# Recurrent cell: the part copies of the key halves issued from GpSimd's queue, those of the query halves from SyncE's

## The reference, cut to what matters

```
log_f = jax.nn.log_sigmoid(fg)
cs = jnp.cumsum(log_f, axis=1)
log_D = where(mask, cs[:, :, None] - cs[:, None, :], -inf) + ig[:, None, :]
max_log_D = jnp.max(log_D, axis=-1, keepdims=True)
D_mat = jnp.exp(log_D - max_log_D)
qk = jnp.einsum('hsd,htd->hst', qh, kh) / np.sqrt(DH)
C = qk * D_mat
normalizer = jnp.maximum(jnp.abs(C.sum(axis=-1, keepdims=True)), jnp.exp(-max_log_D))
h = jnp.einsum('hst,htd->hsd', C / (normalizer + EPS), vh)
return (h - mu) / jnp.sqrt(var + LN_EPS) * ln_scale
```

## Time and profile before

| what | us |
|---|---|
| median of 3 runs | 6493.87 |
| lowest and highest of them | 6456.07 and 6500.29 |
| the profiled execution | 6481.38 |
| its span | 6479.7 |
| the cell stage in it, from GpSimd's first instruction to VectorE's last | 3149.1 to 3470.5 |

### The profile page before, as it was taken

The page is one execution under the profiler, slowest core; times in us unless marked ns, Lnnn a source line. Parts: engine busy times, 40 slices in busy tenths (PEclk is TensorE's granted clock), DMA queues, the critical chain, the costliest instruction groups (busy, mean ns, idle before and its releaser), DMA issues. The chain is left out here.

```text
span 6479.7 us, 102180 instructions
## 1 busy us (share of the span) xinstructions
PE 4692.1 (72%) x24710; PEld 2851.4 (44%) x24710; DVE 3959.5 (61%) x8261; ACT 2814.7 (43%) x5978; POOL 2018.5 (31%) x3020
## 2 busy tenths in 40 slices
PE   7446666391787973797675767697677687995897
PEld 4113333240353322687233645486555574333533
DVE  6335555637546876444387966557866455886565
ACT  2235555114314762322453556434556332772353
POOL 0114443000006641222343554124553113552342
PEclk9557889695897987898777989898889898997897
DMA  4999996100034330210452232002321006332543
GB/s 157 301 323 194 184 185 149 50 0 0 0 115 133 90 75 20 70 43 23 128 157 59 109 113 74 29 7 78 133 74 46 26 16 200 91 86 60 181 124 97
DMA packets 372621, 648.43 MB, mean 100 GB/s; under 512 B 78834, under 2 KB 182931, under 8 KB 372200
## 3 DMA queue, kind: packets, MB, share of 16 engines
q1 hardware_dynamic: 300728, 450.70, 22.9%
q0 software_dynamic: 71488, 193.32, 12.4%
HBM read 373.99 MB, written 238.70 MB: 95 GB/s over the span
## 5 line engine op out<-in xcount | busy, mean ns | idle before, releaser
L1115 DVE TENSOR_REDUCE t_nmax<-t_aps 128x2 f32<-128x1024 f32 x700 | 837.6, 1222 | 281.9 <-PE t_aps L1037 276.4
L1222 ACT ACTIVATE t_expT<-t_bps 128x512 f32<-128x512 f32 x1290 | 701.7, 599 | 288.2 <-PE t_bps L1056 237.8
L1056 PE MATMUL t_bps<-t_Q,t_K 51*128 51x512 f32 (+2 forms) x1290 | 528.9, 472 | 59.4 <-ACT t_expT L1222 43.3
L1037 PE MATMUL t_aps<-t_K,t_Q 49*128 49x512 f32 (+2 forms) x1400 | 467.7, 462 | 64.7 <-DMA t_K<-k_halves 29.4
L1056 PEld LDWEIGHTS t_bps<-t_Q,t_K 51*128 51x128 f32 (+2 forms) x1290 | 230.2, 190 | 528.6 <-ACT t_expT L1222 374.2
L2474 DVE TENSOR_TENSOR f_hl<-f_h,f_hh 128x512 fp32r<-128x512 f32 x192 | 203.9, 1062 | 412.4 <-ACT f_hh L2399 412.4
L3882 ACT ACTIVATE t_relsb<-t_relsb,t_nmax 128x128 f32<-128x128 f32 (+3 forms) x515 | 280.3, 561 | 317.4 <-DVE t_nmax L3855 314.1
L1083 PE MATMUL t_ops<-t_expT,t_V 128*17 128x512 f32 (+1 forms) x2560 | 416.6, 618 | 0.4 <-ACT t_expT L1222 0.4
L3816 PE MATMUL t_tps<-ident,t_relsb 128*128 128x128 f32 x1280 | 266.8, 317 | 173.5 <-ACT t_expT L3701 165.2
L2762 POOL TENSOR_TENSOR a_crossed<-a_qsb,a_tab 128x256 f32<-128x256 f32 x272 | 268.0, 1007 | 299.7 <-ACT a_qsb L2709 272.1
L3855 DVE CUSTOM_DVE_ANT_0 t_relsb<-t_sps,t_relsb 128x128 f32<-128x128 f32 (+3 forms) x515 | 235.5, 485 | 138.2 <-POOL t_relsb L3781 86.5
(11 more groups left out here) (431 smaller groups left out, 12493.6 us busy)
## 6 DMA issues: line engine op xcount, KB each, us to landing
rel<-r_out SPq DMA_DIRECT2D x128, 640.0 KB, 5.4
t_relsb<-rel SPq DMA_DIRECT2D x128, 256.0 KB, 4.6
t_Q<-q_halves POOLq DMA_DIRECT2D x420, 64.0 KB, 2.5
t_K<-k_halves POOLq DMA_DIRECT2D x420, 64.0 KB, 2.6
t_relsb<-rel SPq DMA_DIRECT2D x128, 192.0 KB, 3.6
k_halves<-a_parts SPq DMA_DIRECT2D x48, 512.0 KB
q_halves<-a_parts SPq DMA_DIRECT2D x48, 512.0 KB, 5.5
t_relsb<-rel SPq DMA_DIRECT2D x128, 128.0 KB, 3.5
```

The source lines that it names most:

```text
L1037: last = nc.tensor.matmul(aps[:, (t * PPG + i) % 2, x, :], operand(Qr, KA, p, h, slice(t * P, (t + 1) * P)), operand(Kr, KA, p, h, slice(0 ...
L1056: nc.tensor.matmul(bps[:, slot_of(kb, j), :], operand(Kr, KB, p, h, slice(kb * P, (kb + 1) * P)), operand(Qr, KB, p, h, slice(0, S)), star ...
L1115: nc.vector.tensor_reduce(nmax[:, g, t, i * HPT:(i + 1) * HPT], aps[:, (t * PPG + i) % 2], AX.X, ALU.max, negate=True).then_inc(s["maxed"], 1)
L1222: nc.scalar.activation(expT[:, kb % RING, j, :], bps[:, slot_of(kb, j), :], ACT.Exp).then_inc(s["expo"], 1 + (PAD if end else 0))
```

## The change

The twelve copies of a set that write `K` (8 of `Kh`, 4 of `Kl`) leave SyncE's queue for GpSimd's; the twelve that write `Q` stay. Each kind gets semaphores of its own (`parts0/1`, `kparts0/1`), and TensorE waits for both. GpSimd issues the copies of parts(b, 0) after `keys(b)` and ahead of the diagonal of pair 3, and those of parts(b, 1) after the diagonal and maxima of pair 0 and ahead of the diagonal of pair 1. ScalarE's `Qh` waits for the copies of Q alone, `Kh` and GpSimd's `Kl` for those of K alone.

```diff
-    PARTS = 6 * HH * 16
+    PARTS = 3 * HH * 16
...
-                    for made, dst, src, terms in (("qh", Q, Qh, (0, 1)), ("kh", K, Kh, (0, 2)), ("ql", Q, Ql, (2,)), ("kl", K, Kl, (1,))):
+                    for made, dst, src, terms in (("qh", Q, Qh, (0, 1)), ("ql", Q, Ql, (2,))):
...
                 def keys(b):
                     pool.wait_ge(s["kh"], b + 1)
-                    wait(pool, "parts1", b * PARTS)
+                    wait(pool, "kparts1", b * PARTS)
...
+                def parts(b, half):
+
+                    if b or half:
+                        wait(pool, "score", ((b - 1) * HP + 2 + 2 * half) * NT)
+                    for made, dst, src, terms in (("kh", K, Kh, (0, 2)), ("kl", K, Kl, (1,))):
+                        pool.wait_ge(s[made], b + 1)
+                        for j in range(HH):
+                            for r in terms:
+                                pool.dma_start(dst[r * DH:(r + 1) * DH, half, j, :], src[j * DH:(j + 1) * DH, half, :]).then_inc(s[f"kparts{half}"], 16)
...
                 keys(0)
+                parts(0, 0)
                 pool.wait_ge(s["tri"], 1)
                 for g in range(NP):
                     b, i = pair(g)
                     diagonal(g)
                     maxima(g + 2)
+                    if i == 0:
+                        parts(b, 1)
                     if i == 2 and b + 1 < NB:
                         queries(b + 1)
                         keys(b + 1)
+                        parts(b + 1, 0)
                     if i == 3 and b:
                         spread(b - 1)
...
                         pe.wait_ge(s[f"parts{i // 2}"], (b + 1) * PARTS)
+                        pe.wait_ge(s[f"kparts{i // 2}"], (b + 1) * PARTS)
...
-                    wait(act, "parts1", b * PARTS)
+                    wait(act, "kparts1", b * PARTS)
```

More of the change, by code:

```diff
@@ L2994, in cell @@
     RING = 3
-    PARTS = 6 * HH * 16
-    with phase(nc, name, "w c0 c1 qh kh ql kl parts0 parts1 vt vcp vones m0 m1 m2 diag d score ct zero pv kept turned lg den0 den1 den2 normed bn stats held rstd centred out tri tri0") as (s, sb, ps):
+    PARTS = 3 * HH * 16
+    with phase(nc, name, "w c0 c1 qh kh ql kl parts0 parts1 kparts0 kparts1 vt vcp vones m0 m1 m2 diag d score ct zero pv kept turned lg den0 den1 den2 normed bn stats held rstd centred out tri tri0") as (s, sb, ps):
         cT = sb("cT", [P, 2, KT, S])
```

## The result

| | kernel before | changed kernel |
|---|---|---|
| median, lowest and highest of 20 runs each | 6484.93 (6456.07 to 6514.83) | 6510.35 (6485.54 to 6544.65) |
| profiled execution, its span | 6481.38, 6479.7 | 6505.1, 6503.4 |
| cell stage in it | 321.4 | 337.0 |
| VectorE's wait between the stage and the next one | 1.83 | 8.33 |

The changed kernel takes 1.0041 times as long, 95% interval 1.0028 to 1.0054: some 27 us more, 18 to 35 by the interval. That is slower, but inside the 1% at which this text draws its line. 6510 was measured and 6512 predicted, but the agreement is largely luck. The forecast stood on a median of 3 runs of the kernel before, 6494, and 20 runs give 6485; so the baseline was 9 us too high and the step, +18 forecast and +25 measured by the medians, 7 us too small. And part of that step went where the prediction did not look.

The account below looks back on a forecast made before the run. The cell stage was taken as a ring of waits through SyncE's issues and GpSimd's queue. Turns +19.1, start +1.0 and end -2.2 made +18 us on a median of 6494: 6512 us, range 6467 to 6550.

Parts of the forecast that it names:

- What bounds the kernel: Cell stage: a chain of waits, with SyncE's issues (15.2 of 38.3 us a turn) and GpSimd's queue on the ring.
- The price of an issue: GpSimd's queue: 0.52 us for each copy issued, 6.2 us for a set of twelve.
- Rival B: GpSimd issues cost twice as much beside VectorE: +96 us on top of the +18, 6608 us; chance 0.08.
- The set for pairs 2 and 3: GpSimd, ahead of pair 1's diagonal: diagonal ready at T0+8.8, `Qh` at T0+15.4 instead of T0+16.6, 1.2 us left.
- T0: Moment when the last scores of a batch are done, which releases the next part copies; a turn runs between two.
- The set for pairs 0 and 1: GpSimd, ahead of the spread: it ends 16.8 us after `Qh`, VectorE idles 6.3, 25.2 us to next T0.
- rival C: The turn stays the same, VectorE or TensorE absorbing half the delay: 0 to +8 us, 6494 to 6502; chance 0.17.
- Sum of a turn: Batch cycle: 15.4 + 25.2 = 40.6 us against 38.3; six turns 243.6 us against 224.5, +19.1.
- The start: Before the first turn: last scores come at 3202.2, where SyncE began at 3201.2 before; +1.0 us.
- The end: Last batch, only its first half counting: pair 2 begins 2.2 us earlier, -2.2 us.
- Rival A: GpSimd's issues cost the ring nothing: 34.4 us a turn, -27 us, 6467 as a median; chance 0.15 (or between it and nothing).
- Beside the next diagonal, as before: VectorE's add behind the spread: taken as 3.6 us, unchanged, in the 25.2 us from `Qh` to the next T0.

Follow-up runs that it names:

- set0_behind_spread: Changed kernel with the K copies for pairs 0 and 1 issued after the spread instead of ahead of the diagonal of pair 3: 6470.0 us, ratio 0.9970.
- both_behind: Changed kernel with K copies for pairs 0 and 1 after the spread, those for pairs 2 and 3 after the diagonal of pair 1: 6452.26 us, ratio 0.9942.
- after_drain_earlier: Changed kernel with one more DRAIN on GpSimd, in idle time ahead of the last batch's spread: 6506.05 us, ratio 1.0021.
- set1_behind_diagonal: Changed kernel with the K copies for pairs 2 and 3 issued after the diagonal of pair 1 and ahead of the maxima: 6511.28 us, ratio 1.0025.
- both_behind_drain_earlier: both_behind with one more DRAIN on GpSimd ahead of the last batch's spread: 6451.91 us, ratio 0.9933 against the kernel before.
- set1_alone_behind_drain_earlier: Changed kernel, only K copies for pairs 2 and 3 on GpSimd, behind pair 1's diagonal; the others on SyncE; early DRAIN: 6466.77 us, ratio 0.9954.
- k_copies_left_out: Changed kernel with the copies of `Kh` and `Kl` made for batch 0 only: 6452.71 us in one run.

## Why the prediction was right, and where it was not

*What bounds the kernel*: right. The stage is a ring of waits, GpSimd's queue lies on it with almost no slack, and what stands ahead of the diagonal and of the spread is paid for. set0_behind_spread and both_behind show it by moving nothing but the order.

*The price of an issue*: 0.496 us (median) against 0.52, a set 5.9 us against 6.2. Rival B is out: the longest took 0.535, beside VectorE's work. The note of the Trainium skill that the prediction named there (SBUF — State Buffer, the note on DVE blocking DMAs under SBUF: two separate sides) did not bear on these issues by its own condition, and none of the 192 shows such a wait.

*The set for pairs 2 and 3*: diagonal ready and pair 1 begun at T0+8.7 (8.8 predicted), `Qh` at T0+15.1 (15.4). "The old wait is gone" and "what is late next is ScalarE" both hold.

*The set for pairs 0 and 1*: the spread ends 16.1 us after `Qh` (16.8), the tiny operation of the divide is at 0.17 us as said, T0 follows 24.5 us after `Qh` (25.2). The idle time of the add is 8.39 us, not 6.3: the centre ran beside issues and took 1.66 us instead of 3.43, so VectorE was early by that much and waited it out. This was in rival C as a gain. It is none, because the add waits for `rstd` anyway.

*Sum of a turn*: 39.6 us, 40.6 predicted. The six turns took 3440.14 - 3199.73 = 240.4 us, +15.9 instead of +19.1. Five are of 39.6 and one of 42.3: the gap before GpSimd's 129th DMA lies in it. So the turns were 1.0 us shorter than forecast each, and a stop that I did not foresee gave 2.7 us of that back: luck once more.

*The start*: the first T0 came 51.2 us after the stage began, against 52.1 before: -0.9, where I had +1.0.

*The end*: the step "pair 2 begins 2.2 us earlier, -2.2 us" held halfway. The weigh of pair 3 came at T0+26.4 in the last batch, 28.3 before, 1.9 us earlier. But from that T0 to the end of the last add it took 45.4 us against 44.8: the gain was lost behind the weigh, in TensorE's last products. Its timeline, before and then after, and the windows around them:

```profile
3458.47 2.35 PE L3159 MATMUL t_hps<-t_C,t_V 128*33 128x512 f32 x16
```

```profile
3471.68 3.92 PE L3174 MATMUL t_hps<-t_C,t_V 128*33 128x512 f32 x16
```

```profile
3455.00:3465.00 10.00, 7.05 (x46) 3.15 (x45) 7.20 (x25) 0.00 (x0) 0.00 (x0) 0.99 0.00 0
```

```profile
3469.00:3479.00 10.00, 8.08 (x38) 3.50 (x34) 4.80 (x18) 0.00 (x0) 0.00 (x0) 0.67 0.00 0
```

The granted clock was 0.99 there before and 0.67 after, so part of the stretch ran at the lower level; the 16 products alone cost 1.6 us more. Between T0 and that weigh it was the other way round, 0.68 before and 0.86 after. So neither the 1.9 us won nor their loss is the change's alone, and why the clock was granted so in these two executions no run here tells.

*The sum for the stage*: +15.6 measured, +18 predicted, its three terms 15.9, -0.9 and 0.6.

*What was left out*: the prediction said that "a step of time outside the cell stage, where nothing is changed" would show it wrong. There is one, 6.5 us in the hand-over. The change adds 192 DMAs to GpSimd's queue, and I priced their issue and their transfer, not their settling in the DRAIN of the block's end. The row was there to be asked for: the drain took 3.87 us before, with 32 DMAs. after_drain_earlier shows that it is this term: with the debt paid in idle time the hand-over is 0.98 us. With it in, the stage's own +15.6 makes 22, against some 27 (18 to 35) over all runs.

*Rival A*, the issues cost the ring nothing, 6467, did not come true here, because of where the issues stand. But what it said could be won was there, and more than its 27 us: the version without K copies and the one with both sets moved have stages 36 and 38 us shorter than the kernel before. My sentence that only 1.2 of the 7.6 us saved are left hid how much there was to win. The Trainium skill says that issuing from a second engine saves only the sequencer's time, "usually small relative to the DMA itself" (DMA: Bandwidth & Descriptors, Issuing engines are not separate DMA queues). For one copy the trace before agrees: 0.59 us to issue it, 2.4 (median) from there to its landing. For 24 in one queue it does not carry over, since their issues add up to 15.2 us of a turn of 38.3 while the landings overlap.

*"Beside the next diagonal, as before"*: I took the add at 3.63 us as given. It is 1.67 when GpSimd issues beside it. This price, with the 2.94 us of the divide, is also part of what my expectation for set1_behind_diagonal got wrong.

## What to carry to other kernels

When DMA issues move to an engine that also computes, ask of each group what stands behind it in that queue and who waits for it. Here the same 24 issues a batch made the kernel 0.4% slower ahead of a diagonal and a spread, and 0.6% faster behind them. Issues can also act as a spacer: 6 us of them between two of GpSimd's operations kept its adds away from VectorE's add and divide, though in both_behind another of its adds then met the centre. Count the settling of such DMAs at the block's end too, and put a drain where the engine is idle.

## What the runs showed of the hardware

- GpSimd's DRAIN grew by 82 ns for each DMA it had issued since the last one, up to 128 of them (1.23 us with none, 3.87 with 32, 5.82 with 56, 11.70 with 128). Beyond that it was shorter: 4.20 with 160, 10.32 with 224. By the same rate about 124 and 113 had been settled on the way (an estimate). Before the 129th GpSimd stopped for 2.5 to 2.7 us in five of the profiles, for 0.47 in set0_behind_spread, and not at all in both_behind and both_behind_drain_earlier. Small DMAs of 32 rows or of one row, 16 bytes each, gave the same 4.197. A drain in idle time took it over: 10.24 us there and 1.23 at the end in after_drain_earlier, 11.62 and 1.24 in set1_alone_behind_drain_earlier.
- ScalarE's drain was not short either, 3.95 us after, but it ran long before the end and cost nothing.
- Some operations of VectorE took longer beside GpSimd's adds, even a tiny one: 128 x 8 numbers took 0.17 us alone and up to 3.51 beside them (set1_behind_diagonal), an add of four times 128 x 256 took 1.67 and 3.63 (5.00 in k_copies_left_out). Beside GpSimd's DMA issues both ran at their own pace (0.17 and 1.67 in both_behind).
- An issue of a 64 KB copy within SBUF took 0.50 us on GpSimd's queue and 0.59 on SyncE's (medians). The longest were 0.54 and 1.71 in the changed kernel, and 0.59 on GpSimd in set0_behind_spread.
